# State-space stage of a six-block decoder: half of the decays of every second state in PSUM, that state's scan in two halves, and three banks instead of four for the turned states

## The reference, cut to what matters

```python
deltaA  = jnp.exp(jnp.einsum('bld,dn->lbdn', delta, A))        # decays
deltaBu = jnp.einsum('bld,bln->lbdn', delta * u, Bm)           # drive
def step(h, inp):
    dA, dBu, c = inp
    h = dA * h + dBu                                           # scan over the 256 tokens
    return (h, jnp.einsum('bdn,bn->bd', h, c))                 # weighted sum over the 16 states
```

## Time and profile before

| | |
|---|---|
| median of three runs | 3192.54 us |
| the profiled execution | 3200.47 us, of which the span is 3198.7 us |
| state-space stage, first to last scan | 1828.0 to 2450.8 us of the span |
| TensorE, VectorE, GpSimd, ScalarE busy over the span | 90%, 64%, 33%, 48% |
| scans (L2124) | 128, 387.8 us |
| drives (L2077) | 128, 432.4 us |
| sums (L2135) | 256, 176.3 us |

### The profile page before, as it was taken

The page is one execution under the profiler, slowest core; times in us unless marked ns, Lnnn a source line. Parts: engine busy times, 40 slices in busy tenths (PEclk is TensorE's granted clock), DMA queues, the critical chain, the costliest instruction groups (busy, mean ns, idle before and its releaser), DMA issues. The chain is left out here.

```text
span 3198.7 us, 51833 instructions
## 1 busy us (share of the span) xinstructions
PE 2894.7 (90%) x19089; PEld 1902.9 (59%) x19136; DVE 2044.5 (64%) x2560; ACT 1538.8 (48%) x2925; POOL 1064.7 (33%) x951
## 2 busy tenths in 40 slices
PE   7999799888888888889999999999976999989998
PEld 5666456444444444446666777777754656657776
DVE  4787666699999998661110299999997232334444
ACT  3444212489999898641111366666662111114433
POOL 0000044356666565420000177777885000000000
PEclk9999799799999999889999999999986999999999
DMA  2011322288888789640003111111112610200000
GB/s 89 28 33 34 100 73 79 66 162 169 169 169 169 160 167 186 161 137 27 20 19 128 47 47 54 54 53 53 47 47 104 119 38 21 67 20 27 20 20 27
DMA packets 497941, 256.57 MB, mean 80 GB/s; under 512 B 412112, under 2 KB 449616, under 8 KB 496208
## 3 DMA queue, kind: packets, MB, share of 16 engines
q1 hardware_dynamic: 487456, 247.66, 30.7%
q0 software_dynamic: 10288, 6.29, 1.4%
HBM read 121.65 MB, written 33.69 MB: 49 GB/s over the span
## 5 line engine op out<-in xcount | busy, mean ns | idle before, releaser
L1108 DVE TENSOR_REDUCE xh_top<-xh_seen 128x1 f32<-128x512 f32 (+1 forms) x768 | 632.0, 863 | 53.3 <-PE xh_seen L1010 39.6
L1080 ACT ACTIVATE xh_prob<-xh_sc,xh_bias,xh_scale 128x1024 int16<-128x1024 f32 (+1 forms) x512 | 610.3, 1202 | 76.2 <-PE xh_sc L1010 72.5
L2077 POOL TENSOR_TENSOR ss_state<-ss_du,ss_b_all 128x1024 f32<-128x1024 f32 x128 | 432.4, 3389 | 185.2 <-PE ss_turned L1790 111.3
L1010 PE MATMUL xh_seen<-xh_kT,xh_qT 96*128 96x512 bf16 x1024 | 357.8, 392 | 78.3 <-DVE xh_top L1108 75.7
L2124 DVE TENSOR_TENSOR_SCAN ss_state<-ss_decay,ss_state 128x1024 f32<-128x1024 f32 x128 | 387.8, 3030 | 29.0 <-ACT ss_decay L1969 28.7
L1010 PE MATMUL xh_sc<-xh_kT,xh_qT 96*128 96x512 bf16 x1024 | 312.8, 388 | 1.3 <-ACT xh_prob L1080 1.3
L1134 POOL CAST xh_probT<-xh_pairs 128x2048 int16<-128x2048 uint8 x128 | 242.0, 1891 | 17.3 <-DMA xh_pairs<-xh_prob 8.6
L1010 PEld LDWEIGHTS xh_seen<-xh_kT,xh_qT 96*128 96x128 bf16 x1024 | 90.0, 98 | 240.6 <-DVE xh_top L1108 216.2
L1797 PE MATMUL ss_bank<-ss_xc,hold_w_conv 128*128 128x256 f32 x1024 | 229.3, 379 | 0.7 <-ACT ss_xc L1981 0.7
L1969 ACT ACTIVATE ss_decay<-ss_delta,ss_a 128x255 f32<-128x255 f32 x512 | 210.9, 496 | 23.7 <-DVE ss_state L2124 23.3
L1797 PEld LDWEIGHTS ss_bank<-ss_xc,hold_w_conv 128*128 128x128 f32 x1024 | 189.9, 189 | 26.4 <-ACT ss_xc L1981 1.1
(11 more groups left out here) (285 smaller groups left out, 4959.8 us busy)
## 6 DMA issues: line engine op xcount, KB each, us to landing
ss_b_all<-ss_states SPq DMA_DIRECT2D x8, 2048.0 KB, 7.1
xa_kT<-xp_kT SPq DMA_DIRECT2D x8, 768.0 KB, 6.0
xh_qT<-xa_qT SPq DMA_DIRECT2D x48, 128.0 KB, 3.3
xh_kT<-xa_kT SPq DMA_DIRECT2D x48, 128.0 KB, 3.4
sa_x<-in_x SPq DMA_DIRECT2D x8, 512.0 KB, 3.8
sa_y<-in_x SPq DMA_DIRECT2D x8, 512.0 KB, 4.8
x_after_self_attention<-sa_y_out SPq DMA_DIRECT2D x8, 512.0 KB, 3.0
xp_x<-x_after_self_attention SPq DMA_DIRECT2D x8, 512.0 KB, 6.5
```

What stands on the lines that cost most here:

```text
L1010: ins = pe.matmul(out[:, c * D:(c + 1) * D], qT[s][:, t * P:(t + 1) * P], kT[s][:, at + c * D:at + (c + 1) * D], start=True, stop=True)
L1080: act.activation(out, scores, ACT.Exp, bias=bias[t % RING][:, :], scale=scale[s][:, t:t + 1], accum_out=total[s][:, half, t:t + 1]).then_i ...
L1108: ins = v.tensor_reduce(top[t % RING][:, k:k + 1], scores[:, 0:n], AX.X, ALU.max)\
L2077: g.tensor_tensor(state[k % RING][:, :, :], du[s][:, :, :], spread(b_all[s][:, k, :], KD), ALU.mult)\
```

## The change

- `turned` has three banks instead of four. The transposes of a half wait for the sum three halves earlier; `behind_turn` gives that distance (at the start of a sequence it is larger, since 32 halves are not a multiple of three).
- The bank that comes free is `near`, 128 partitions by 2 x 256 values. For odd k ScalarE writes the first two of the four rows of decays there, and the other two into `decay[k % 4]` as before. As there is one `near`, odd k waits for the scan two states back instead of four.
- For odd k VectorE's scan is two instructions of 512 elements: the first reads `near` and the first half of the state, the second the second half of `decay` and of the state. `scanned` is incremented behind the second.
- One more memset of a zero column, for `near`.

```diff
+    TURNED = 3
-        turned = [p.ps(f"turned{i}", [P, D]) for i in range(BANKS)]
+        turned = [p.ps(f"turned{i}", [P, D]) for i in range(TURNED)]
+        near = p.ps("near", [P, KD // 2, S])
+        def behind_turn(k, t):
+            i = k * TB + t
+            if i >= TURNED:
+                return TURNED
+            return i + N * TB - max(j for j in range(N * TB) if j % TURNED == i)
...
-                        r = (k * TB + t) % BANKS
-                        if not (isinstance(q, int) and c < BANKS // TB):
-                            pe.wait_ge(summed, ONE + c * TB + t - BANKS + 1)
+                        r = (k * TB + t) % TURNED
+                        if not (isinstance(q, int) and c * TB + t < TURNED):
+                            pe.wait_ge(summed, ONE + c * TB + t - behind_turn(k, t) + 1)
...
-                    if not (isinstance(q, int) and c < RING):
-                        act.wait_ge(scanned, ONE + c - RING + 1)
+                    ring = RING // 2 if k % 2 else RING
+                    if not (isinstance(q, int) and c < ring):
+                        act.wait_ge(scanned, ONE + c - ring + 1)
                     for m in range(KD):
-                        ins = act.activation(decay[k % RING][:, m, 1:], delta[s][:, m, 1:], ACT.Exp,
-                                             scale=a[:, m, k:k + 1])
+                        into = near if k % 2 and m < KD // 2 else decay[k % RING]
+                        ins = act.activation(into[:, m, 1:], delta[s][:, m, 1:], ACT.Exp, scale=a[:, m, k:k + 1])
...
-                    v.tensor_tensor_scan(flat(state[k % RING][:, :, :]), flat(decay[k % RING][:, :, :]),
-                                         flat(state[k % RING][:, :, :]), 0.0, ALU.mult, ALU.add).then_inc(scanned, 1)
+                    whole, half = slice(0, KD), KD // 2
+                    if k % 2:
+                        first = state[k % RING][:, 0:half, :]
+                        v.tensor_tensor_scan(flat(first), flat(near[:, :, :]), flat(first), 0.0, ALU.mult, ALU.add)
+                        whole = slice(half, KD)
+                    out = state[k % RING][:, whole, :]
+                    v.tensor_tensor_scan(flat(out), flat(decay[k % RING][:, whole, :]), flat(out), 0.0, ALU.mult,
+                                         ALU.add).then_inc(scanned, 1)
```

More of the change, by code:

```diff
@@ L2109, in _ @@
             v.memset(xc[:, :, 0:PAD], 0.0)
-            for r in range(RING):
-                ins = v.memset(decay[r][:, :, 0:1], 0.0)
+            for tile in decay + [near]:
+                ins = v.memset(tile[:, :, 0:1], 0.0)
             ins.then_inc(padded, 1)
@@ L2134, in add_up @@
                         v.wait_ge(turn_ready, ONE + TB * c + t + 1)
-                        v.scalar_tensor_tensor(acc[s][:, t, :], turned[(k * TB + t) % BANKS][:, :], c_t[s][:, t, k:k + 1],
+                        v.scalar_tensor_tensor(acc[s][:, t, :], turned[(k * TB + t) % TURNED][:, :], c_t[s][:, t, k:k + 1],
                                                acc[s][:, t, :], ALU.mult, ALU.add).then_inc(summed, 1)
```

## The result

The changed kernel takes 3254.39 us (median of 4 runs, 3251.51 to 3256.44) against 3193.57 us before. The ratio is 1.0179, 95% interval 1.0166 to 1.0192. In a second group of runs it was 1.0163 (1.0146 to 1.018). It is slower, as forecast, but by 61 us in the first group and 52 in the second, where 26 were forecast; 3254 lies above the range's end of 3248.

A forecast was written before the change was run, and what follows sets the result against it. TensorE and VectorE were taken as both full in full sequences, with VectorE's scans and GpSimd's products excluding each other. Full sequences +20, sequences 0 and 6 +4, clock +3, sequence 7 -1: +26 us, 3219 us, range 3172 to 3248.

The forecast's parts named there:

- m(k): Moment TensorE reaches the second half of turning state k-1; claimed no earlier than 0.87 us after scan(k) ends.
- x(k): End of scan(k) on VectorE, which is the start of the sums behind it.
- ScalarE's shorter lead: Decays of odd k+2 start behind scan(k); 3 us are spare, so it was claimed to cost nothing.
- The four loops: Closed waits making up one round of a full sequence: 79.3 to 85.5 us against 78.40, taken as +4.0.
- The split scan in the full sequences: Odd scans in two halves, claimed to lie beside TensorE's 75.39 us of work; only sequence 7 counted, at -1 us.
- loop 2: m(8) to m(13), through the output product, scans, delta and du: 25.9 to 28.9 us, before 24.6.
- Loop 4: m(4) to m(5), one step: 4.3 us.
- The ring in the light sequences: Three turned banks in sequences 0 and 6, with less TensorE work: half of 4.0 us each, 4 together.
- The ring in the full sequences: TensorE's later turns with three turned banks: 4.0 us in each of five sequences, 20 together.
- pair of states: An even and an odd state on VectorE with the split: 7.94 us at best, 8.98 at worst, instead of 8.62.
- The clock: TensorE's granted clock may fall after new waits at steps 8 and 13: 0.6 us a sequence, 3 together.
- The rival built on the rule: Scans reading PSUM escape GpSimd's lock and TensorE's lead isn't needed: -26 us, 3166 us; chance 0.18.

The follow-up runs named there:

- three banks alone: The kernel before with three banks for the turned states, whole scans and all decays in SBUF: 3239.1 us, 1.0124.
- the split alone: The kernel before with odd scans in two halves, all decays in SBUF, four banks, ScalarE four states ahead: 3227.41 us, 1.0088.
- four turned banks: The changed kernel with four banks for turned states and three for the other products: 1.0042; with the half reading SBUF alone first, 1.0037.
- a lag of one: The changed kernel with both sums of state k-1 behind scan(k), instead of those of k-2: 1.0011; with the half reading SBUF alone first, 0.9956.
- the early sum: The changed kernel with the first sum of state k-2 ahead of scan(k): 1.0005; with the half reading SBUF alone first, 1.0009.

## Why the prediction was wrong in size

**The mechanism was right.** m(k) waits for x(k) + one sum. In the changed kernel x(13) is 2242.43 and m(13) 2243.20, which is 0.77 later (0.87 forecast). The new waits stand inside the turns of steps 4, 8 and 13 where they were placed; those at steps 5 and 11 were not named. The order of the sums alone, with the same three banks, moves the ratio from 1.016 to 1.0005. ScalarE's shorter lead costs nothing, as said (1.0001). Three signs missed in size: TensorE's idle time until a sum rose to 98.7 us, 1.76 times and not more than double; the wait at step 8 is 1.64 us and not 2 or more; full sequences take 85.0 to 87.2 us and not 81 to 84.

The distance at the start of a sequence was misread in the section on the change: `behind_turn` gives 2, 2 and 5 there, so it is shorter for the first two halves. The turn of state 0 waits for the sums of state 15, behind scan(1). In the full sequences TensorE comes later than that anyway and no wait stands at step 1; in sequence 7 the wait there grew from 3.09 to 4.98 us. The forecast has no term for it.

**The four loops, forecast and measured.** The changed kernel in the round from m(8) = 2213.70 to m(8) = 2298.72, three banks alone in the same round of its own trace:

| loop | forecast, us | three banks alone, us | changed kernel, us |
|---|---|---|---|
| m(8) to m(13) | 25.9 to 28.9 | 27.9 | 29.5 |
| m(13) to m(4) | 33.9 to 35.4 | 36.1 | 35.4 |
| m(4) to m(5) | 4.3 | 4.4 | 5.0 |
| m(5) to m(8) | 15.2 to 16.9 | 15.1 | 15.1 |
| round | 79.3 to 85.5, taken 82.4 | 83.5 | 85.0 |

**The sequences,** from one delta row to the next (sequence 7: from the last delta row to the end of the last scan), with the mean granted clock:

| sequence | before, us (clock) | three banks alone, us | changed kernel, us (clock) | grown by | forecast |
|---|---|---|---|---|---|
| 0 | 69.1 (1.00) | 71.7 | 71.0 (0.98) | 1.9 | 2 |
| 1 | 77.2 (1.00) | 86.8 | 87.2 (0.98) | 10.1 | 4.6 |
| 2 | 79.9 (0.98) | 83.5 | 86.5 (0.98) | 6.6 | 4.6 |
| 3 | 78.5 (1.00) | 83.5 | 85.0 (1.00) | 6.5 | 4.6 |
| 4 | 79.6 (0.98) | 83.5 | 85.0 (1.00) | 5.4 | 4.6 |
| 5 | 78.4 (1.00) | 83.5 | 85.0 (1.00) | 6.6 | 4.6 |
| 6 | 79.5 (0.97) | 82.8 | 85.4 (0.96) | 5.9 | 2 |
| 7 | 86.1 (0.66) | 93.2 | 91.7 (0.69) | 5.6 | -1 |

That is 49 us for the stage, of 51 in the span. The other 2 us are in other stages, and no run looks into them. Against the 26 forecast, three terms of the sum were too small, and they are the steps that failed.

1. **The split scan in the full sequences, put at nothing.** The prediction says that there it "lies beside TensorE's 75.39 us of work" and doesn't enter the loops, but for loop 2. The changed kernel differs from three banks alone by near, the split and ScalarE's wait, which costs nothing. The difference of the two traces is 8.1 us over the five full sequences and 8.5 in the stage; by the ratios, 1.0163 and 1.0179 against 1.0124, it is 12 to 18 us in all. Loop 4, which had no blocked scan in it, grew from 4.4 to 5.0 us with a wait of 0.41 us for the sum behind the blocked second half of scan(5). The assumption is wrong with four banks too: the split alone costs 28 us, since a full sequence already waited for VectorE at step 14. With near the split is worth -1.5 us in sequence 7 of these two traces, so the -1 forecast there was about right; the miss is in the sequences that were left out.
2. **The ring in the light sequences, put at 4 us.** Three banks alone cost 2.6 us in sequence 0, 3.3 in 6 and 7.1 in 7, which is 13.0 together. Sequence 7 had nothing for the ring in the sum, as one "where TensorE has time to spare". But the output product stands behind the turns in TensorE's queue and is late with them. The changed kernel waits for it twice in sequence 7, 0.99 and 3.60 us, and the kernel before didn't. In the whole stage VectorE waits 33.4 us for the output product, 15.8 before.
3. **The ring in the full sequences, taken at 4.0 us each, 20 in all.** Three banks alone cost 27.2 in all, 5.4 each. Here only the size was off: the loops do not close in their middle.

The longer of the two waits named in 2:

```profile
2476.60 0.69 DVE L2167 TENSOR_TENSOR ss_y<-ss_bank,ss_y 128x512 f32<-128x512 f32 x1 [3.60 <-PE ss_bank L1825]
```

Loop 2 passed its range (29.5 against 28.9) by two things together. The blocked second half of scan(13) was in the range, with up to 2.2 us: it took 1.5 (2.71 against 1.19 to 1.20 us for a free one), and three banks alone, with a whole scan there, don't have it. What the loop left out is that GpSimd also blocks the statistics operation (1.42 us instead of 0.17) and the delta operation (2.04 instead of the 1.21 of the row that the forecast took), 2.1 us together. Three banks alone show both of these.

The forecast's upper end of +55 us held 9 for the clock that were not spent. That the measured 52 to 61 us lie near it is in part luck. The ends of its pair of states, 7.94 and 8.98 us, don't follow from the terms that it gives: 1.13 + 1.13 + 1.30 + 4.31 would be 7.87.

**The clock** cost nothing more in the full sequences. In either kernel it fell for a time from 2.4 to 1.2 GHz, the lower of its two levels, in two of the five rows of the table (2 and 4 before, 1 and 2 after: mean 0.98), and such a row is 1.2 to 1.5 us longer than the next one at 1.00. The rows behind the wait of 2.84 us at step 13 are of usual length at a clock of 1.00. The 3 us of the sum were not spent.

**The other terms.** Halves that read near take 1204 to 1225 ns in all 64 cases: free of the lock, as the rule of the Trainium skill (SBUF — State Buffer, "Who interferes with whom") says of an instruction with at most one SBUF input outside the two-port modes. The trace agrees, with 1211 against 1822 ns for first halves that read SBUF alone in the version that lacks near and nothing else. The statistics operation has one input too and was blocked. The rival built on the rule, that the kernel would be faster, was wrong all the same. Near only gave back some 28 of the 82 us that ring and split cost together.

**What stays open.** Why ring and split cost 2.6% together and 2.1% as a sum of their own. The traces show where: in sequence 5 the split adds 5.0 us to three banks alone, 1.9 from m(13) to m(4), 1.3 from m(4) to m(5) and 1.9 from m(5) to m(8). With four banks it adds 3.9, all from m(13) to m(4). No run shows why each scan falls together with a product as it does. Why sequence 1 grew by 10.1 us is open in part: it was the shortest of the full ones before, its clock fell after the change alone, and three banks alone make 9.7 of the 10.1. near with four turned banks and four others was not tried, as it needs nine banks.

## What to carry to other kernels

When a ring is cut by one, look up which instruction makes the release that is now waited for and where it stands in its engine's queue. Here moving that one instruction ahead of a scan took back 1.6%, with no bank more.

Where two engines exclude each other, splitting an instruction in two is not free even if nothing else changes: the other engine gets in between. The order of the parts can matter. With the part that needs the shared resource first and the free part last, the time fell by 0.6% in the changed kernel and by 0.5% with a lag of one, and not at all with the early sum or with four turned banks.

When the time of an engine "beside" the bound is written off, check that the bound engine doesn't wait for it already, and doesn't begin to by the same change. A wait at the end of each round, as at step 14 here, says that it does.

## What the runs showed of the hardware

- One scan of 1024 elements made into two of 512 costs 0.54 us a time against the mean of all scans before (3.57 against 3.03 us), and 0.70 against the same odd scans (2.87). The fixed cost of the second instruction is 0.06 us of that, by the starts of free rows: 1.13 + 1.12 us for two halves, 2.19 for a whole. The rest is waiting for GpSimd's product.
- A whole scan that has begun keeps GpSimd's product waiting (3.82 us instead of 2.36); a product that has begun keeps the next half waiting (2.71 us instead of 1.19).
- A statistics operation of 128x2 elements with one SBUF input took 1.42 us instead of 0.17 beside GpSimd's product, and ended with it.
- A scan that reads its decays from PSUM is as fast as a free one that reads SBUF: 1204 against 1205 ns for the shortest first half of 512 elements, and 1190 against 1190 for the shortest second half.
- ScalarE writes the same 255 exponentials in 459 ns (median, 452 to 479) to PSUM and 492 ns (489 to 513) to SBUF. The Trainium skill (ScalarE: Activation LUTs, "Step-by-step: what each stage is for") says that a write to PSUM is faster; the trace agrees, by 33 ns an instruction.
